# Three of four input products of a selective state-space layer move from VectorE to GpSimd, with a buffer for each

## The reference, cut to what matters

```
xc          = silu(conv4(W_in x))                       # 512 x 128
dt, B, C    = split(W_xproj xc)                         # 16, 16 and 16 rows x 128
delta       = softplus(W_dt dt + b_dt)                  # 512 x 128
h[d,n,t]    = exp(-exp(A_log[d,n]) * delta[d,t]) * h[d,n,t-1] + (delta[d,t] * xc[d,t]) * B[n,t]
y[d,t]      = (sum over n of h[d,n,t] * C[n,t] + D[d] * xc[d,t]) * silu(gate[d,t])
x           = x + W_out y
```

## Time and profile before

| | |
|---|---|
| median of 3 runs | 2614.59 us (2613.96 to 2615.21) |
| span of the profiled execution | 2616.1 us |
| VectorE busy | 1836.6 us, 70% |
| TensorE busy | 2329.4 us, 89% |
| ScalarE busy | 1195.5 us, 46% |
| GpSimd busy | 518.4 us, 20% |
| the selective layer | from about 1998 to 2074 us of the span |

### The profile page before, as it was taken

The page is one execution under the profiler, slowest core; times in us unless marked ns, Lnnn a source line. Parts: engine busy times, 40 slices in busy tenths (PEclk is TensorE's granted clock), DMA queues, the critical chain, the costliest instruction groups (busy, mean ns, idle before and its releaser), DMA issues. The chain is left out here.

```text
span 2616.1 us, 57464 instructions
## 1 busy us (share of the span) xinstructions
PE 2329.4 (89%) x21928; PEld 1442.4 (55%) x21930; DVE 1836.6 (70%) x2821; ACT 1195.5 (46%) x2045; POOL 518.4 (20%) x300
## 2 busy tenths in 40 slices
PE   3999989999994969999987999999996459999979
PEld 2444446666654936666656645655664425555548
DVE  6889778988886176666634488888886777777721
ACT  4566543333334337777772333333332316555552
POOL 0555530000000030000001155555551010000000
PEclk7999989999997969999997999999997669999989
DMA  7676855566534766667625322222221256676644
GB/s 270 215 248 232 273 176 155 168 170 197 168 125 165 216 154 160 159 157 168 158 60 180 124 99 99 98 98 98 98 73 60 65 131 148 156 158 149 147 139 165
DMA packets 245681, 397.64 MB, mean 152 GB/s; under 512 B 28905, under 2 KB 210288, under 8 KB 245396
## 3 DMA queue, kind: packets, MB, share of 16 engines
q1 hardware_dynamic: 239860, 393.90, 52.7%
q10 hardware_dynamic: 5664, 1.44, 0.2%
HBM read 316.44 MB, written 78.06 MB: 151 GB/s over the span
## 5 line engine op out<-in xcount | busy, mean ns | idle before, releaser
L1629 DVE CUSTOM_DVE_ANT_0 l3x_junk<-l3x_pm,l3x_mrow,l3x_top 128x896 bf16<-128x896 f32 x224 | 246.2, 1148 | 89.9 <-PE l3x_pm L1785 89.3
L1713 ACT ACTIVATE l1x_prob<-l1x_ring,mask_col 128x512 f32<-128x512 f32 x392 | 248.1, 685 | 119.3 <-PE l1x_ring L1805 118.3
L1716 ACT ACTIVATE l3x_prob<-l3x_ring 128x512 f32<-128x512 f32 x392 | 213.3, 595 | 162.4 <-PE l3x_ring L1809 162.4
L1163 ACT ACTIVATE l0x_att_pt<-l0x_att_pt 128x1024 f32<-128x1024 f32 x99 | 104.7, 1058 | 255.1 <-DVE l0x_att_pt L1098 255.1
L2778 POOL TENSOR_TENSOR l2x_gk<-l2x_f,first_vin 128x1024 f32<-128x1024 f32 x98 | 184.3, 1916 | 161.1 <-DVEq L2519 161.1
L1208 PE MATMUL l0x_att_pv<-l0x_wv,l0x_att_vin 128*128 128x512 f32 x392 | 195.2, 621 | 0.0
L2652 PE MATMUL l2x_kf<-l2w_w,l2x_nin 128*128 128x512 f32 x392 | 173.5, 602 | 4.4 <-DVE l2x_f L2493 4.4
L2652 PE MATMUL l2x_kf<-l2w_w,l2w_first 128*128 128x512 f32 x392 | 171.1, 596 | 0.0
L2493 DVE SCALAR_TENSOR_TENSOR l2x_f<-l2x_kf,l2x_rs,l2w_bias 128x1024 f32<-128x1024 f32 x98 | 125.8, 1284 | 57.8 <-PE l2x_kf L2652 45.5
L1629 DVE CUSTOM_DVE_ANT_0 l1x_junk<-l1x_pm,l1x_mrow,l1x_top 128x896 bf16<-128x896 f32 x112 | 123.7, 1148 | 57.3 <-PE l1x_pm L1785 57.3
L1629 DVE CUSTOM_DVE_ANT_0 l1x_junk<-l1x_pm,first_mrow,l1x_top 128x896 bf16<-128x896 f32 x112 | 123.4, 1148 | 54.6 <-PE l1x_pm L1785 54.6
(11 more groups left out here) (733 smaller groups left out, 4965.2 us busy)
## 6 DMA issues: line engine op xcount, KB each, us to landing
first_kt<-scratch_KS SPq DMA_DIRECT2D x84, 448.0 KB, 9.2
scratch_KT<-l0x_max_kf SPq DMA_DIRECT2D x28, 896.0 KB, 4.8
l0x_att_kt<-scratch_KT SPq DMA_DIRECT2D x56, 448.0 KB, 6.9
scratch_KS<-l0x_side_kp SPq DMA_DIRECT2D x14, 1344.0 KB, 13.5
l1x_kt<-scratch_KS SPq DMA_DIRECT2D x42, 448.0 KB, 9.7
scratch_KS<-first_kt SPq DMA_DIRECT2D x14, 1344.0 KB, 6.0
l3x_kt<-scratch_KS SPq DMA_DIRECT2D x42, 448.0 KB, 9.1
l0fw_w<-L_ffn_exp_w SPq DMA_DIRECT2D x16, 1024.0 KB, 7.6
```

What stands on the lines that cost most here:

```text
L1629: dve.tensor_tensor_reduce(junk[x % 2][:, :, :], pm[x % 2][:, :, 0:SPLIT], mrow[b][:, :].rearrange("p (s k) -> p s k", s=2), 1.0, top[1 - ...
L1713: ins = act.activation(into, scores, ACT.Exp, bias=R.mask_col[:, bass.ds(m * TILES + n // 4, 1)])
L1716: ins = act.activation(into, scores, ACT.Exp)
```

## The change

There are four `drive` buffers instead of two. VectorE makes only the first product; GpSimd gets a block of its own in this layer, waits until `u` is written (a new semaphore "input", raised by VectorE right after `u`) and until `bc` has landed, and makes the products for blocks 1 to 3 one after the other. Each adds one to a new semaphore "driven", for which VectorE waits before the scan of that block.

```diff
-        drive = [S.sb(f"drive{b}", [P, STATES, P]) for b in range(2 if selective else 0)]
+        drive = [S.sb(f"drive{b}", [P, STATES, P]) for b in range(IC if selective else 0)]
...
                     link(dve.tensor_tensor(u[:, :, :], delta[:, :, :], xc[:, :, :], ALU.mult))
+                    dve.sem_inc(S.sem("input"), 1)
...
-                def driven(c):
-                    link(dve.tensor_tensor(drive[c % 2][:, :, :], wide(u[:, c, :]), bc[:, 0:STATES, :], ALU.mult))
-
                 if selective:
-                    driven(0)
+                    link(dve.tensor_tensor(drive[0][:, :, :], wide(u[:, 0, :]), bc[:, 0:STATES, :], ALU.mult))
                 for c in range(IC):
                     b = c % 2
-                    if selective and c + 1 < IC:
-                        driven(c + 1)
+                    if selective and c:
+                        dve.wait_ge(S.sem("driven"), c)
                     if c >= 2:
                         dve.wait_ge(S.sem("summed"), c - 1)
                     if selective:
                         dve.wait_ge(S.sem("decay"), STATES * (c + 1))
-                        link(dve.tensor_tensor_scan(flat(state[b]), flat(decay[c]), flat(drive[b]), 0.0, ALU.mult,
+                        link(dve.tensor_tensor_scan(flat(state[b]), flat(decay[c]), flat(drive[c]), 0.0, ALU.mult,
                                                     ALU.add))
...
+            if selective:
+                @block.gpsimd
+                def _(pool):
+                    pool.wait_ge(S.sem("input"), 1)
+                    pool.wait_ge(S.sem("bc"), 16)
+                    for c in range(1, IC):
+                        pool.tensor_tensor(drive[c][:, :, :], u[:, c, :].unsqueeze(1).broadcast_to([P, STATES, P]),
+                                           bc[:, 0:STATES, :], ALU.mult).then_inc(S.sem("driven"), 1)
```

## The result

The changed kernel took 2620.13 us in the median of 16 runs, the kernel before 2614.28 in 16 runs beside it: ratio 1.0022 with an interval of 1.0015 to 1.003, so 5.85 us slower. The forecast was 2620.1.

What follows compares the result with a forecast made beforehand. VectorE was taken to bound the selective layer's stage. The first scan 10.0 us later, against 4.5 gained in the loop, gave net +5.5: 2614.6 + 5.5 = 2620.1 us, range 2616.5 to 2622.6.

Steps and rivals of the forecast that it cites:

- Start and length of GpSimd's work: Ahead of the first scan: GpSimd starts at 2026.6; its three products take 4.50 us each, 13.5 in all.
- rival 3: A GpSimd product takes 3.61 us instead of 4.50: +2.8 us, 2617.4; chance 0.04.
- The skips: VectorE's four skips ahead of the first scan, 0.87 us alone, are blocked by GpSimd's products: first 3.8, later about 4.4.
- The row of 1.94: Earlier trace: one-scalar VectorE operation, 128x8, takes 0.23 us alone, 1.94 beside GpSimd; taken to show skips are blocked.
- that of 0.41: Earlier trace: two-scalar VectorE operation took 0.41 us inside a GpSimd instruction; by it the skips would not take turns.
- rivals 1 and 2: 1: no turns, products hidden, -5.2 us, chance 0.07; 2: skips not blocked, scans take turns, +4.5 us, chance 0.06.
- First scan: Starts at 2042.6 instead of 2032.61, 10.0 us later, after GpSimd's three products, the skips and VectorE's first product.
- turns at the port: VectorE and GpSimd alternate whole instructions at the shared SBUF port; one turn of both takes 2.84 us for 3.12 alone.
- The loop: From first scan to end of last multiply: 27.7 us instead of 32.2, scans 6.96 apart, a gain of 4.5.
- The tail: TensorE's last block of sums behind the last multiply: 3.84 us at full clock, left unchanged.
- Rival 4: As forecast, but TensorE's last block at half clock, up to 2.5 us more: +8.0, 2622.6; chance 0.05.
- The sum: First scan 10.0 us later against 4.5 gained in the loop: net +5.5 us, 2620.1 us; chance 0.78.

Runs made afterwards that it cites:

- the spare products: Kernel before, all four products still on VectorE, plus three GpSimd products into buffers nobody reads: 2626.18 us, ratio 1.0052.
- the late start: Changed kernel with "input" raised behind VectorE's own product instead of behind `u`, so GpSimd's products fall beside the scans: 2621.47 us, ratio 1.0033.
- the pair with and without PSUM: Kernel before, skips and gate product moved ahead, block 2's product in halves on GpSimd: scan states in PSUM 2612.54 us, in SBUF 2615.8 us.
- the one product: Kernel before with only block 3's product moved to GpSimd: 2617.16 us, ratio 1.0009.
- each fill of 1.8 us: Kernel before in its own order, plus six GpSimd memsets of spare buffers from the end of `u`: 2619.97 us in one run.
- the control: Kernel before, skips and gate product moved ahead, block 2's product in two GpSimd halves, scan states in SBUF, not PSUM: 2615.8 us, ratio 1.0004.

## Why the prediction was right

By its steps, times counted from the end of `u`:

- **Start and length of GpSimd's work.** Forecast: 0.2 us behind `u`, 4.50 a product. Measured 0.13 (2025.79) and 4.50 to 4.51. The choice of 4.50 over 3.61, by which operand is full, was right, and rival 3 fell.
- **The skips.** Forecast: held, the first for 3.8 us, later ones for about 4.4. Measured 3.86, 4.54, 4.55 and 0.27. The row of 1.94 was the right neighbour and that of 0.41 the wrong one; rivals 1 and 2 fell with it.
- **First scan.** Forecast 10.0 us later, measured 9.90 (16.09 against 6.19). The cause, turns at the port and not a wait, was an inference from three rows; the spare products, the late start and the pair with and without PSUM show it.
- **The loop.** Forecast a gain of 4.5, measured 4.07 (28.09 instead of 32.16). This is the term that was mis-sized. From scan to scan it took 6.97, 7.00 and 7.37, not 6.96. The idle time ahead of the fourth scan, 0.61 us instead of 0.21, is nearly all of the difference, and it is not the wait on "summed": the block that it asks for, the second, ended at 2055.59 + 3.84 = 2059.43, over 3 us earlier. Nor is it "driven" (GpSimd ended at 2039.24), nor a decay (ScalarE's last one ended at 2045.03). The kernel with the late start has the same 0.61 at the same place, the others have 0.25 at most; what it is stays open.
- **The tail.** Left unchanged, and it was: 3.99 in both profiles. Rival 4 was real as a mechanism, but not here: the changed kernel's medians (+5.85) leave nothing for it beyond the stretch (+5.83). Of the eleven kernels' profiles two have a slow last block, the late start (6.59) and the one product (5.47), and their medians lie 1.7 and 2.1 us above what their stretches add. Whether it belongs to these orders or to single executions, one profile of each can't tell.
- **The sum.** +5.5 forecast, +5.83 in the stretch: 0.4 from the loop, less 0.1 from the first scan. That the time itself came out at 2620.13 against 2620.1 is luck beyond this: the kernel before measured 2614.28 beside it, 0.3 us under the 2614.59 that the forecast was added to, and that offset took up the difference. The page's busy times alone (VectorE 70%, GpSimd 20%) would have had it the other way round.

## What to carry to other kernels

Before work goes from VectorE to GpSimd, ask what VectorE does meanwhile: beside a GpSimd operation that reads SBUF, each VectorE operation with two SBUF inputs, and each one-tensor operation like the skips, can wait out a whole GpSimd instruction. The move then costs GpSimd's duration (4.5 us) for VectorE's own (2.3), even where nobody waits for the result. Here it paid beside VectorE work with an operand in PSUM, in pieces about as long as that work (2.36 us beside 2.29); other lengths were not tried.

## What the runs showed of the hardware beyond what I expected

- A held instruction counts as busy. The skips show 12.99 us for 0.87 of work, with no idle time and no wait named; only a mean far above that of the same form elsewhere gives it away.
- Not every one-tensor operation is held: that with two scalars in the earlier trace rows wasn't, the skips with one were. The kind of GpSimd instruction isn't the difference. Some 3 us later in the trace of before, an operation with one scalar (0.23 alone) is held until the same GpSimd operation of line 3362 ends; no run tried one form against the other.

```profile
1406.15 2.84 POOL L3362 TENSOR_SCALAR l2w_w<-l2w_w,l2w_g 128x1024 f32<-128x1024 f32 x1
1408.12 0.89 DVE L189 TENSOR_SCALAR l1f_pr<-l1f_lg,l1f_sw 128x8 f32<-128x8 f32 x1
```

- How many short operations pass beside one GpSimd instruction differs: one skip for each product of 4.5 us (3.86, 4.54, 4.55), but two for each fill of 1.8 us (four skips in 3.08 us). The fills wait for each other by a semaphore, and some 0.05 us lie between two of them; the products follow with none. Whether that is the reason is open.
- Which engine is first is settled by tenths of a microsecond: 0.11 us made the multiply hold GpSimd's half in the control, and the half then held the scan. The Trainium skill, SBUF — State Buffer, "Who interferes with whom", says that the order of issue decides who blocks; these rows agree.
- A scan that writes 128x2048 to PSUM takes 4.43 us against 4.42 to SBUF, and a multiply that reads it from there the same 2.29.
